# A two-layer graph network: the second layer all dense, and a chunk's gathers held for the landing of the preceding chunk's tiles

## What is computed

```python
h = relu(layernorm(x))                              # x: 6250 nodes x 96
ea = edge_attr @ W_edge.T + b_edge                  # 200000 edges x 96
msg = relu(h[src] + ea)
aggr = segment_sum(msg, dst, 6250)
x = x + relu(((1 + eps) * h + aggr) @ W1.T + b1) @ W2.T + b2
...
h = relu(layernorm(x))
m = relu(h[src]) + 1e-7
ex = exp(m - segment_max(m, dst)[dst])
a = ex / segment_sum(ex, dst)[dst]
x = x + (h + segment_sum(a * m, dst)) @ W + b
```

## Time and profile before

| | us |
|---|---|
| median of 3 runs | 3177.6 (3171.68 to 3183.03) |
| profiled execution, its own time | 3172.46 |
| its span, first to last instruction | 3170.7 |
| busy: PE, DVE, POOL, ACT | 2043.8, 1922.5, 1740.9, 762.9 |
| mean granted TensorE clock | 0.778 of full speed |
| moved by DMA | 322.5 MB |

### The profile page before, as it was taken

The page is one execution under the profiler, slowest core; times in us unless marked ns, Lnnn a source line. Parts: engine busy times, 40 slices in busy tenths (PEclk is TensorE's granted clock), DMA queues, the critical chain, the costliest instruction groups (busy, mean ns, idle before and its releaser), DMA issues.

```text
span 3170.7 us, 45342 instructions
## 1 busy us (share of the span) xinstructions
PE 2043.8 (64%) x11221; PEld 1635.3 (52%) x11222; DVE 1922.5 (61%) x4523; ACT 762.9 (24%) x1322; POOL 1740.9 (55%) x1820
## 2 busy tenths in 40 slices
PE   3466666666666666666656676666666674777778
PEld 1255555555555555555545555555555563455556
DVE  7466666666666666666666666666667871233334
ACT  4000011112222222333333333334343550000000
POOL 5356666566666666666666666666666104444441
PEclk8677777777777777777787777777777876788889
DMA  4122333333333333334333343332222155455443
GB/s 134 22 59 70 81 76 79 79 89 93 91 87 94 94 105 96 98 99 108 107 100 105 107 115 103 109 105 71 62 62 62 39 161 175 158 164 164 162 162 119
DMA packets 152071, 322.53 MB, mean 102 GB/s; under 512 B 65291, under 2 KB 106027, under 8 KB 137791
## 3 DMA queue, kind: packets, MB, share of 16 engines
q1 hardware_dynamic: 27286, 151.94, 16.2%
q0 software_dynamic: 61632, 100.73, 13.9%
q10 hardware_dynamic: 63014, 68.51, 6.4%
HBM read 247.64 MB, written 73.38 MB: 101 GB/s over the span
## 4 chain that ended last, share of the span: by engine, by line
DVE 27%; PE 21%; another core or an unknown queue 21%; issue 18%; DVEq 6%; ACT 1%; DMA 0%; SPq 0%; ACTq 0%
DVE zone L1369 14%; PE ps L849 11%; DVE planes L1140 5%; DVE ps L1341 5%; PE ps L775 4%; PE ps L659 3%; DVEq L1369 2%; PE ps L859 1%; DVEq L374 1%; PE ps L646 1%; DVE planes L1146 1%; PE ps L680 1%; DVE features_buf L1354 1%; DVE onehot L1140 1%
## 5 line engine op out<-in xcount | busy, mean ns | idle before, releaser
L564 POOL DMA_INDIRECT rows_buf<-table,index x1563 | 1503.0, 962 | 944.0 <-remote 426.0
L775 PE MATMUL ps<-zone,planes 128*128 128x400 f16 x2352 | 682.7, 411 | 852.2 <-DVE zone L1369 662.3
L775 PEld LDWEIGHTS ps<-zone,planes 128*128 128x128 f16 x2352 | 268.4, 114 | 1036.2 <-issue 976.7
L992 ACT ACTIVATE features_buf<-ps 128x800 f16<-128x800 f32 x392 | 328.2, 837 | 1696.3 <-PE ps L775 829.7
L1369 DVE TENSOR_SCALAR zone<-iota_c,planes 128x400 f16<-128x400 int16 x2352 | 686.0, 345 | 56.2 <-issue 52.1
L659 PEld LDWEIGHTS ps<-wet,zone 128*128 128x128 f32 x3136 | 625.0, 279 | 49.2 <-issue 45.2
L659 PE MATMUL ps<-wet,zone 128*128 128x96 f32 x3136 | 601.0, 358 | 0.0
L1341 DVE TENSOR_TENSOR ps<-ps,rows_buf 128x768 f32<-128x768 f32 x195 | 187.5, 962 | 494.1 <-remote 447.2
L646 PE MATMUL ps<-onehot,features_buf 128*96 128x128 f32 x3120 | 478.9, 305 | 1.5 <-issue 1.5
L646 PEld LDWEIGHTS ps<-onehot,features_buf 128*96 128x96 f32 x3120 | 446.6, 193 | 20.9 <-issue 7.8
L1140 DVE TENSOR_TENSOR onehot<-ps,dstf 128x1024 f32<-128x1024 f32 x196 | 239.1, 1220 | 228.8 <-remote 224.8
(11 more groups left out here) (184 smaller groups left out, 778.6 us busy)
## 6 DMA issues: line engine op xcount, KB each, us to landing
zone<-edge_t SPq DMA_DIRECT2D x98, 768.0 KB
counts<-features_buf ACTq DMA_DIRECT2D x288, 200.0 KB
rows_buf<-counts SPq DMA_DIRECT2D x24, 1600.0 KB
rows_buf<-table,index POOLq DMA_INDIRECT x1563
planes<-counts SPq DMA_DIRECT2D x12, 1600.0 KB
table<-planes SPq DMA_DIRECT2D x5, 840.0 KB
final<-residual ACTq DMA_DIRECT2D x48, 48.0 KB
out<-final ACTq DMA_DIRECT2D x48, 48.0 KB
```

Source lines behind the costliest of these rows:

```text
L564: nc.gpsimd.indirect_dma_start(out=into[:, t, :], out_offset=None, in_=table, in_offset=bass.IndirectOffsetOnAxis(ap=at[:, t:t + 1], axis= ...
L775: nc.tensor.matmul(count_ps[:, bass.ds(banks[k], WC)], row_hot[:, u % 2, g * GS + k, :], pair_hot[:, g * GS + k, :], start=False, stop=Fal ...
L992: nc.scalar.activation(count_out[:, k], bank, ACT.Copy, accum_out=row_sum[:, bass.ds(p, 1)]).then_inc(moved, 1)
```

## The change

1. The second layer has no fetched blocks: all 49 are dense, in their order. ACT stores all 392 pairs of counts; the stores of the weighted table, the gathers and one-hots of the second layer, the loads of edge ends and the part of the check that goes with them are gone.
2. The gathers of a chunk are issued in one go of eight. Ahead of them GpSimd waits until seven of the eight tiles of the preceding chunk have landed (also in the first eight chunks), and, from the ninth chunk on, for `ea_done` of chunk c - 7. The eighth tile counts on a semaphore of its own, `last_in`, for which the add waits too. The waits for `add_done` and `sum_done` are gone.

```diff
-LOTS = [range(0, 3), range(3, 6), range(6, 8)]
+TL = T - 1
...
-            def gather(into, table, at, signal, tiles=range(T)):
-                for t in tiles:
+            def gather(into, table, at, signal, last, tiles=T):
+                for t in range(tiles):
                     nc.gpsimd.indirect_dma_start(
                         out=into[:, t, :], out_offset=None, in_=table,
-                        in_offset=bass.IndirectOffsetOnAxis(ap=at[:, t:t + 1], axis=0)).then_inc(signal, 16)
+                        in_offset=bass.IndirectOffsetOnAxis(ap=at[:, t:t + 1], axis=0)).then_inc(signal if t < TL else last, 16)
...
-            def chunk_rows(i, u, lots=LOTS):
+            def chunk_rows(i, u, paced=True, tiles=T):
                 c = i * IS + u
-                pool.wait_ge(add_done, c + 1)
+                if u:
+                    pool.wait_ge(rows_in[(u - 1) % RS], i * (2 * 16 * TL) + ((u - 1) // RS + 1) * (16 * TL))
+                if paced:
+                    pool.wait_ge(ea_done, c - (RS - 2))
                 if u % RS == 0:
                     pool.wait_ge(index_in[u % IS // RS], (i + (u // IS + 1)) * 16)
                 pool.sem_inc(gathers_begun, 1)
-                rows_of(u, lots[0])
-                if len(lots) > 1:
-                    pool.wait_ge(ea_done, c - (RS - 2))
-                    pool.sem_inc(gathers_begun, 1)
-                    rows_of(u, lots[1])
-                    pool.wait_ge(sum_done, c + (NS + 1 - RS))
-                    pool.sem_inc(gathers_begun, 1)
-                    rows_of(u, lots[2])
+                gather(rows[:, u % RS], table0, index[:, u % IS], rows_in[u % RS], last_in[u % RS], tiles)
...
             for u in range(RS):
-                chunk_rows(0, u, [range(T)])
+                chunk_rows(0, u, False)
...
-            with pool.Else():
-                pool.wait_ge(fetch_in, GB * 16)
-                pool.wait_ge(own_out, 2 * NU * 16)
-                pool.wait_ge(weighted_out, 2 * NU * 16)
-                for g in range(GB):
-                    if g >= 2:
-                        pool.wait_ge(block_ps, 2 + ORDER.index(DB + g - 2) + 1)
-                    gather(fetched[g % 2], weighted, fetch_ends[:, 0, FETCH_AT[g]:FETCH_AT[g + 1]], fetched_in[g % 2],
-                           range(FETCH[g]))
...
                 for s in range(2, NB):
-                    if ORDER[s] < DB:
-                        block_sums(s, ORDER[s])
-                    else:
-                        fetched_sums(s, ORDER[s] - DB)
+                    block_sums(s, s)
...
-                for b in range(3, DB):
-                    sp.wait_ge(block_ps, 2 + ORDER.index(b - 3) + 1)
+                for b in range(3, NB):
+                    sp.wait_ge(block_ps, b)
                     block_load(b)
...
-            with act.Fori(0, KEPT // OB) as i:
+            with act.Fori(0, NPAIR // OB) as i:
                 needed = load(act, ready, i * OB, OB, [SC + NSTEP] * OB)
                 for k in range(OB):
-                    close(i * OB + k, k, needed[k], True)
+                    close(i * OB + k, k, needed[k])
...
-                dve.wait_ge(rows_in[u % RS], rounds * (16 * T))
+                dve.wait_ge(rows_in[u % RS], rounds * (16 * TL))
+                dve.wait_ge(last_in[u % RS], rounds * 16)
```

More of the change, by code:

```diff
@@ L65 @@
 FEAT = 5760
[L66 to L76, removed]
 NE = 4
@@ L314, in gnn_kernel @@
         rows_in = [sem(f"rows_in{u}") for u in range(RS)]
+        last_in = [sem(f"last_in{u}") for u in range(RS)]
         x_index = [sem(f"x_index{h}") for h in range(2)]
@@ L415, in by_tile @@
             return buf.bitcast(dt).rearrange("p (q e) -> p q e", q=QT)
-        def fetched_before(g):
-            return 16 * sum(FETCH[g % 2:g:2])
-        weighted, own_rows = table1.bitcast(F16), table0
+        own_rows = table0
         def wait_high(engine, u):
@@ L516, in _ @@
                     own_store(u)
-                weighted_store(0)
-                weighted_store(1)
-                own_store(NU - 2)
-                weighted_store(2)
-                own_store(NU - 1)
+                for u in range(NU - 2, NU):
+                    own_store(u)
                 block_load(2)
-                weighted_store(3)
                 sp.wait_ge(own_out, 2 * NU * 16)
@@ L593, in _ @@
                 chunk_rows(0, u)
-            chunk_rows(0, NC - 1, [range(T_END)])
+            chunk_rows(0, NC - 1, tiles=T_END)
             with pool.If(fast_of(pool) < 1):
@@ L852, in block_sums @@
                     last.then_inc(block_ps, 1)
-                def fetched_sums(s, g):
-                    pe.wait_ge(fetched_in[g % 2], fetched_before(g + 2))
-                    pe.wait_ge(fetch_hot_done, g + 1)
-                    pe.wait_ge(soft_done, s + 1)
-                    for k in range(FETCH[g]):
-                        last = nc.tensor.matmul(ps[:, s % 2, 0:4 * D], fetch_hot[g % 2][:, k, :],
-                                                fetched[g % 2][:, k, :], start=(k == 0), stop=(k == FETCH[g] - 1))
-                    last.then_inc(block_ps, 1)
                 def turn(b, u):
@@ L1003, in _ @@
             act.wait_ge(meta_ready, 1)
-            with act.Fori(0, KEPT // OB) as i:
+            with act.Fori(0, NPAIR // OB) as i:
                 needed = load(act, ready, i * OB, OB, [SC + NSTEP] * OB)
                 for k in range(OB):
-                    close(i * OB + k, k, needed[k], True)
+                    close(i * OB + k, k, needed[k])
             for k in range(OB):
-                act.wait_ge(stored[k], (KEPT // OB + 1) * 16)
-            with act.Fori(KEPT // OB, NPAIR // OB) as i:
-                needed = load(act, ready, i * OB, OB, [SC + NSTEP] * OB)
-                for k in range(OB):
-                    close(i * OB + k, k, needed[k], False)
+                act.wait_ge(stored[k], (NPAIR // OB + 1) * 16)
             deviation_of(1, 0)
```

115 lines of the change are left out of this document (15 added, 100 removed).

## The result

The changed kernel takes 3046.8 us (median of 4 runs, 3043.8 to 3059.5), the kernel before 3178.5 us on the same chip (4 runs). The ratio is 0.9595, 95% interval 0.9562 to 0.9628: 4% faster, where 14% was forecast. The profiled execution took 3059.5 us, with a span of 3057.7; it is the longest of the four, 13 us over the median, where that of the kernel before is 6 us under its own. One execution in all that follows, one of the dense layer alone on chip 2, took 9362 us for an unknown reason and is in no ratio.

A forecast was written before the change was run, and what follows sets the result against it. It took long unbroken gather streams on GpSimd, holding back other engines' signals, to bound the kernel. 3172.5 - 296 (first layer) - 148 (second layer) + 3 (stores) - 1 (checks) = 2730, median 2735 us; range 2660 to 3010.

The forecast's parts named there:

- The second layer: Second layer all dense: 406 us in place of 548, so -142; residual lands 6 us earlier; layer -148.
- its cover: Second layer's dense loads: hidden behind 8.44 us blocks, costed at nothing; if not, 11.4 us a block, +139 us.
- The new stores: Last seven chunks: ACT also issues the added stores and waits for the one four back; 0 to 10 us, taken as 3.
- The pause's size: First layer, between bursts of eight gathers: gaps of about 1.15 us instead of 2.41, a round 11.0 us.
- From there each pause releases one signal, the chunk's period is the round's: First layer's chunks after the start: adds 11.0 us apart instead of 12.3; -296 us with the start's 52 included.
- with a pause after each eight gathers the masks should go at their early pace: Start: 26 masks in 9 us plus 4 us of copies instead of 59.4; first add from 162.3 to about 110.
- the next mask wait until 127.67: Start, kernel before: after the last gather the next mask still waits 4.8 us; some 6 us of waiting should fall away.
- Rival (a): First layer: GpSimd stays slot-bound, rounds remain 12.3 us; only start (-52) and second layer (-148) gain; 2980 us, chance 0.33.
- Rival (c): First layer: landings seen as late as TensorE's signals, 4.9 us; round 14.2 us, slower than before at 3360 us; chance 0.07.

The follow-up runs named there:

- the dense layer alone: Changed kernel with a chunk's gathers again in three lots behind the old waits, so only the dense second layer is left: 0.9536 on chip 2, 1.019 on chip 4.
- all eight: Changed kernel with all eight tiles on one semaphore, each chunk awaiting the landing of the whole preceding one: 0.9375 (2948 us) on chip 2, 1.268 on chip 5.
- the first four: Experiments on chip 2: the dense layer alone 0.9536; changed kernel with a second landing wait mid-chunk 0.9668; without landing wait 0.9819; all eight 0.9375.
- the start's pauses alone: Full landing waits only ahead of the first eight chunks, chip 5: added to the dense layer alone 1.028, to the changed kernel 1.140, to the kernel before (chunks 1-7) 1.007.
- mixed pauses: Changed kernel awaiting all eight tiles ahead of chunks 0 to 7 and even chunks, seven ahead of odd ones: 1.241 on chip 3, 1.242 on chip 5.

## Why the prediction was wrong

The sign was right and the size wrong: 2735 forecast, 3046.8 measured, outside 2660 to 3010. The sign is the second layer's alone.

- **The second layer** (-142 and -6): -144.0 and -9.8. Right, with its cover: the copies are 8.43 us apart, so the loads hide. The new stores (3): +5.4.
- **The pause's size:** right. Where only the landing is waited for, gaps are mostly 1.0 to 1.5 us against 1.15 forecast.
- **The step that failed:** "From there each pause releases one signal, the chunk's period is the round's", and at the start "with a pause after each eight gathers the masks should go at their early pace". I had read of before that a pause releases what was held 1.65 us after the burst, and then priced a pause of 1.15 us, which ends before that, as if it did too. In the trace the pauses of 1.0 to 1.4 us release too little: start -3.8 in place of -52, so that chunk 8 finds its slot taken, and from there the slots bind, chunks +39.2 in place of -244. With pauses of 2.3 us the start did move, to 114 (all eight, chip 2).
- **A reading beside it:** the prediction has the next mask wait until 127.67, after the last gather. In the trace of before five masks run from 121.10 to 122.86, right behind the gathers; the wait of 4.8 us is that of the sixth.
- **Rival (a),** the slots bind, is what happened on chip 1, at 0.33. It was 67 us too low, since it too had the start's 52 us, and took its rounds for those of before, where they are 0.21 us longer.
- **Rival (c)'s** mechanism, a landing seen late, shows on chip 1 in five pauses of 3.6 to 4.2 us only. On chips 3 to 5, where waits of 4 to 6 us stand behind edge loads, it is a part of the loss.
- **What no step could hold:** that the trace's main feature, held signals, belongs to the chip, or the hour, that it was taken on. On chip 4 both halves of the change lose (1.019 for the dense layer, 1.147 with the pacing), and what was run of either on chips 3 and 5 agrees.

The Trainium skill, "DMA: Bandwidth & Descriptors", section "Rules for kernel authors", says to issue a transfer early and wait for it late. Chips 4 and 5 agree, at 1.6 us a chunk for a wait right behind the issue (2.3 us and more where all eight are awaited). On chip 2 the same wait for all eight is the fastest of four variants, since there the opening that it gives the other engines at the start is worth more.

## What to carry to other kernels

A pause meant to let others through has to be priced against the release seen in the trace (here 1.65 us after the last gather of eight) and not by the wait's own length; or the burst has to be so short that nothing is held in it (here four gathers, at the start). A wait behind each issue costs its full length as soon as the issuing engine is the bound, and its landing can fall behind a large load. Before tuning against idle time with an unnamed releaser, time the unchanged kernel on a second chip: here the best pacing for one chip was 27% slower than before on another.

## What the runs showed of the hardware

- One program took 3178 us on chip 1, 3142 us on chip 2 and 2461 to 2466 us on chips 3 to 5; in each set its runs agree to 0.5%.
- What is late on the first two is at least TensorE's semaphore updates, by the times at which the traces have them. The earlier trace rows is one: the product ends at 1508.82, the update of `ea_done` is recorded at 1513.69, and the add starts at 1513.71. While GpSimd gathers, 1250 of 2286 recorded updates of TensorE come over 1 us after the instruction that makes them in the kernel before on chip 1, and 1208 of 2252 in the dense layer alone on chip 2; in the 14 traces of chips 3 to 5 none of some 2800 each does. Of VectorE's and ScalarE's recorded updates none does in any trace; but on chips 1 and 2 a third of theirs have no record, so what became of those isn't known. Half of the late `ea_done` are recorded within 0.1 us of 1.7 us after a burst's end (before, chip 1).
- There a stream of gathers takes effect after some length. At the start, from 61.6 to 109 us, 15 of 23 recorded updates of TensorE are late in the kernel before, 8 of 35 with bursts of eight and pauses of 1.0 us (chip 1), 1 of 64 with pauses of 2.3 us and none of 53 in bursts of four with pauses of 1.0 us (chip 2). In the rounds that follow, all of them have late ones again.
- Whether instructions on their way to the engines are held as well stays open: idle time is put down to "remote", up to 6.6 us at once in the masks of the changed kernel, and to "issue", 10.9 us in those of the dense layer alone on chip 2. So does why two chips do this. Whether it is the chip itself or something beside it at that time was not tried either: no chip is known to have been used in both conditions, and no experiment after the first four met the first kind again. So the start's pauses alone, and mixed pauses, are untested there.
- No version was found that beats both kernels on both kinds of chip; of those that ran on both, the dense layer with the old lots loses least (0.954 and 1.019).
